# Second attention of a two-layer cross-attention kernel: keys spread over 64 features at a time, scores and maxima products as pairs of 64-row tiles

## The reference, cut to what matters

```python
q = (Q @ Wq_w + Wq_b).reshape(b, tq, H, DK).transpose(0, 2, 1, 3)   # H 16, DK 8
k = (K @ Wk_w + Wk_b).reshape(b, tk, H, DK).transpose(0, 2, 1, 3)
v = (V @ Wv_w + Wv_b).reshape(b, tk, H, DK).transpose(0, 2, 1, 3)
scores = jnp.einsum('bhqd,bhkd->bhqk', q, k) / jnp.sqrt(jnp.float32(DK))
scores = jnp.where(mask == 0, jnp.float32(-1000000000.0), scores)
attn = jax.nn.softmax(scores, axis=-1)
out = jnp.einsum('bhqk,bhkd->bhqd', attn, v)
out = out.transpose(0, 2, 1, 3).reshape(b, tq, c)
return out @ Wo_w + Wo_b
```

## Time and profile before

| what | value |
|---|---|
| median of 3 runs (lowest to highest) | 856.46 us (855.76 to 857.66) |
| profiled execution, its own time | 855.94 us |
| its span, first to last instruction | 854.1 us |
| PE busy / weight loads | 751.2 us (88%) / 625.1 us (73%) |
| DVE, ACT, POOL busy | 598.6 us (70%), 419.9 us (49%), 426.8 us (50%) |
| mean granted TensorE clock, share of full speed | 0.951 |
| second attention | from about 495 us to about 763 us of the span |

### The profile page before, as it was taken

How to read it: one execution, slowest core, us unless ns; L and a number is a source line. 1 busy time by engine, 2 the same in 40 slices (tenths; PEclk the granted TensorE clock), 3 DMA queues, 4 the chain that set the end, 5 groups by cost and what they waited for, 6 DMA issues and landing times. The chain is left out here.

```text
span 854.1 us, 24200 instructions
## 1 busy us (share of the span) xinstructions
PE 751.2 (88%) x9170; PEld 625.1 (73%) x9170; DVE 598.6 (70%) x1658; ACT 419.9 (49%) x847; POOL 426.8 (50%) x464
## 2 busy tenths in 40 slices
PE   3699999999999999999999559999999999966666
PEld 2488878888887888788877437888888888844343
DVE  4576678766876687667864346676776767669996
ACT  2344454445454544444543114555455554537877
POOL 3575557555765567456752043444444444345440
PEclk9799999999999999999999757999999999987988
DMA  9200000000000000000000000000000000000001
GB/s 257 78 2 9 10 10 2 7 7 7 0 7 7 7 0 7 7 7 0 0 2 2 2 11 4 10 6 8 4 4 7 4 7 0 1 2 13 26 25 38
DMA packets 23388, 12.98 MB, mean 15 GB/s; under 512 B 6144, under 2 KB 22480, under 8 KB 23344
## 3 DMA queue, kind: packets, MB, share of 16 engines
q1 hardware_dynamic: 22528, 12.02, 5.2%
q10 hardware_dynamic: 816, 0.36, 0.1%
HBM read 10.28 MB, written 2.10 MB: 14 GB/s over the span
## 5 line engine op out<-in xcount | busy, mean ns | idle before, releaser
L517 POOL TENSOR_TENSOR a_turned<-a_turned,a_rope 128x512 f32<-128x512 f32 x64 | 81.9, 1280 | 166.9 <-DVE a_turned L601 166.9
L745 ACT ACTIVATE a_probs<-bank 77x512 f32<-77x512 f32 x128 | 70.8, 591 | 65.4 <-PE bank L895 64.5
L1462 PE MATMUL bank<-a_q,a_keys 128*128 128x128 f32 x640 | 93.6, 286 | 0.0
L598 DVE TENSOR_TENSOR a_straight<-bank,a_rope 128x512 f32<-128x512 f32 x64 | 44.1, 689 | 61.8 <-PE bank L825 57.3
L518 POOL TENSOR_TENSOR a_qr<-a_straight,a_turned 128x512 f32<-128x512 f32 x64 | 82.3, 1286 | 5.0
L726 ACT COPY a_vs<-bank 77x512 f32<-77x512 f32 x64 | 37.3, 582 | 95.6 <-PE bank L825 95.6
L1462 PEld LDWEIGHTS bank<-a_q,a_keys 128*128 128x128 f32 x640 | 81.1, 196 | 0.1
L626 DVE TENSOR_REDUCE a_am<-bank 128x6 bf16<-128x462 f32 (+1 forms) x96 | 50.3, 581 | 37.6 <-PE bank L869 37.6
L891 PE MATMUL bank<-a_qr,a_kr 64*77 64x128 f32 x1024 | 71.0, 278 | 2.3 <-ACT a_probs L745 0.6
L891 PEld LDWEIGHTS bank<-a_qr,a_kr 64*77 64x77 f32 x1024 | 56.3, 145 | 17.0 <-ACT a_fold L740 9.0
L907 PE MATMUL bank<-a_vs,a_probs 77*64 77x65 f32 x2048 | 66.8, 223 | 0.0
(11 more groups left out here) (226 smaller groups left out, 1965.5 us busy)
## 6 DMA issues: line engine op xcount, KB each, us to landing
a_ctx_in<-in_ctx SPq DMA_DIRECT2D x32, 77.0 KB
out<-x_all SPq DMA_DIRECT2D x8, 256.0 KB, 2.3
x_all<-in_x_dram SPq DMA_DIRECT2D x7, 256.0 KB, 5.8
a_mask_in<-in_mask SPq DMA_DIRECT2D x16, 77.0 KB
a_wq<-in_Wq SPq DMA_DIRECT2D x1, 512.0 KB, 4.9
a_wk<-in_Wk SPq DMA_DIRECT2D x1, 512.0 KB, 6.4
a_wv<-in_Wv SPq DMA_DIRECT2D x1, 512.0 KB, 7.5
a_wo<-in_Wo SPq DMA_DIRECT2D x1, 512.0 KB, 8.7
```

The lines of the kernel that those rows point to most:

```text
L517: steps.link(nc.gpsimd.tensor_tensor(tv, tv, rope[:, 1:2, :].broadcast_to([128, 4, S]), ALU.mult))
L745: nc.scalar.activation(probs[:, 4 * g:4 * g + 4, :], ps[ST_BANK[g]][0:KL, :].rearrange("p (h s) -> p h s", s=S), ACT.Exp).then_inc(s_free[ ...
L1462: nc.tensor.matmul(ps[g][:, (tile % 4) * S:(tile % 4 + 1) * S], keys[P][:, j, 128 * tile:128 * tile + 128], q1[P][:, j, :], start=tile % 4 ...
```

## The change

The mask `BLK` now repeats every 64 features, and `keys` shrinks from 1280 to 640 columns: columns 0 to 511 hold, in features 0 to 63, keys 0 to 63 of heads 0 to 7, and in features 64 to 127 those of heads 8 to 15; columns 512 to 639 do the same for the last 13 keys. The spreads of DVE and POOL and the casts of ACT are over half the columns. Each product of queries and keys now runs over 64 rows, `lo` (features 0 to 63, bank 0) or `hi` (64 to 127, bank 1), and half of bank 2 each. In `score_maxima` the three mask products come first, then the four key products; in `scores` all ten key products come first, then all ten of `fold_w`. A new semaphore `half_done` keeps the two halves from writing bank 2 together.

```diff
-    blk = (rows[:, None] // DK1 == np.arange(H1)[None, :]).astype(np.float32)
+    blk = (rows[:, None] // DK1 % 8 == np.arange(8)[None, :]).astype(np.float32)
...
-    keys = [sb(f"keys{i}", [D, 2, 10 * 128], F32) for i in range(2)]
-    keysb = [sb(f"keysb{i}", [D, 2, 10 * 128], BF16) for i in range(2)]
+    keys = [sb(f"keys{i}", [D, 2, 5 * 128], F32) for i in range(2)]
+    keysb = [sb(f"keysb{i}", [D, 2, 5 * 128], BF16) for i in range(2)]
...
+    FEATURES = (slice(0, D // 2), slice(D // 2, D))
...
         engine.tensor_tensor(
-            keys[P][:, j, 0:1024].rearrange("p (h k) -> p h k", k=KM),
-            k1[:, j:j + 1, 0:KM].broadcast_to([D, H1, KM]),
-            BLK.rearrange("p (h a) -> p h a", a=1).broadcast_to([D, H1, KM]), ALU.mult)
+            keys[P][:, j, 0:512].rearrange("p (h k) -> p h k", k=KM),
+            k1[:, j:j + 1, 0:KM].broadcast_to([D, 8, KM]),
+            BLK.rearrange("p (h a) -> p h a", a=1).broadcast_to([D, 8, KM]), ALU.mult)
         return engine.tensor_tensor(
...
@@ -1439,14 +1440,21 @@
-                nc.tensor.matmul(out, t["identb"][:], mask_cols, start=True, stop=False)
-                nc.tensor.matmul(ps[i][:, 0:cols.stop - cols.start], q1b[P][:, j, :], keysb[P][:, j, cols],
-                                 start=False, stop=True).then_inc(s_full[i], 1)
+                nc.tensor.matmul(out, t["identb"][:], mask_cols, start=True, stop=False, skip_group_check=True)
+            lo, hi = FEATURES
+            nc.tensor.matmul(ps[2][:, 0:128], q1b[P][lo, j, :], keysb[P][lo, j, 512:640],
+                             start=False, stop=True, skip_group_check=True).then_inc(half_done, 1)
+            nc.tensor.matmul(ps[1][:], q1b[P][hi, j, :], keysb[P][hi, j, 0:512],
+                             start=False, stop=True, skip_group_check=True).then_inc(s_full[1], 1)
+            nc.tensor.matmul(ps[0][:], q1b[P][lo, j, :], keysb[P][lo, j, 0:512],
+                             start=False, stop=True, skip_group_check=True).then_inc(s_full[0], 1)
+
+            pe.wait_ge(half_done, 2 * b + 1)
+            nc.tensor.matmul(ps[2][:, 128:256], q1b[P][hi, j, :], keysb[P][hi, j, 512:640],
+                             start=False, stop=True, skip_group_check=True).then_inc(s_full[2], 1)
...
@@ -1456,15 +1464,22 @@
+            def score(g, i, half, tile, first):
+                return nc.tensor.matmul(ps[g][:, i * S:(i + 1) * S], keys[P][FEATURES[half], j, 128 * tile:128 * tile + 128],
+                                        q1[P][FEATURES[half], j, :], start=first, stop=False, skip_group_check=True)
+
+            score(2, 0, 0, 4, True).then_inc(half_done, 1)
+            for i in range(4):
+                score(1, i, 1, i, i == 0)
+                score(0, i, 0, i, i == 0)
+
+            pe.wait_ge(half_done, 2 * b + 2)
+            score(2, 1, 1, 4, False)
+
+            pe.wait_ge(fold_ready, b + 1)
             for g in range(3):
                 tiles = range(4 * g, 4 * g + (4 if g < 2 else 2))
-                for tile in tiles:
-                    nc.tensor.matmul(ps[g][:, (tile % 4) * S:(tile % 4 + 1) * S],
-                                     keys[P][:, j, 128 * tile:128 * tile + 128], q1[P][:, j, :],
-                                     start=tile % 4 == 0, stop=False, skip_group_check=True)
-                if g == 0:
-
-                    pe.wait_ge(fold_ready, b + 1)
```

More of the change, by code:

```diff
@@ L103, in later_weights @@
                    bv=sb("a1_bv", [S, 1, D], F32), bo=sb("a1_bo", [S, 1, D], F32),
-                   fold_w=sb("a1_fold_w", [FOLD, 10, 128], BF16), blocks=sb("a1_blocks", [128, 26], F32),
+                   fold_w=sb("a1_fold_w", [FOLD, 10, 128], BF16), blocks=sb("a1_blocks", [128, 18], F32),
                    mask=sb("a1_mask", [S, KL], I32))
@@ L1038, in layer1_attention @@
     s_full, s_free = [sem(f"s_full{i}") for i in range(3)], [sem(f"s_free{i}") for i in range(3)]
-    m_full, fold_ready, maxima_ready = sem("m_full"), sem("fold_ready"), sem("maxima_ready")
+    m_full, fold_ready, maxima_ready, half_done = sem("m_full"), sem("fold_ready"), sem("maxima_ready"), sem("half_done")
     qk_ready, vals_in, vals_ready = sem("qk_ready"), sem("vals_in"), sem("vals_ready")
@@ L1052, in layer1_attention @@
     HALVES = (slice(0, S // 2), slice(S // 2, S))
-    BLK, HALF, EIGHTH = (blocks[:, 0:16], blocks[:, 16:18], blocks[:, 18:26])
+    BLK, HALF, EIGHTH = (blocks[:, 0:8], blocks[:, 8:10], blocks[:, 10:18])
+    FEATURES = (slice(0, D // 2), slice(D // 2, D))
     def pairs_loop(engine, slot, steps=None, per=0):
@@ L1081, in spread @@
         engine.tensor_tensor(
-            keys[P][:, j, 0:1024].rearrange("p (h k) -> p h k", k=KM),
-            k1[:, j:j + 1, 0:KM].broadcast_to([D, H1, KM]),
-            BLK.rearrange("p (h a) -> p h a", a=1).broadcast_to([D, H1, KM]), ALU.mult)
+            keys[P][:, j, 0:512].rearrange("p (h k) -> p h k", k=KM),
+            k1[:, j:j + 1, 0:KM].broadcast_to([D, 8, KM]),
+            BLK.rearrange("p (h a) -> p h a", a=1).broadcast_to([D, 8, KM]), ALU.mult)
         return engine.tensor_tensor(
-            keys[P][:, j, 1024:1280].rearrange("p (h k) -> p h k", k=RPAD)[:, :, 0:KR],
-            k1[:, j:j + 1, KM:KL].broadcast_to([D, H1, KR]),
-            BLK.rearrange("p (h a) -> p h a", a=1).broadcast_to([D, H1, KR]), ALU.mult)
+            keys[P][:, j, 512:640].rearrange("p (h k) -> p h k", k=RPAD)[:, :, 0:KR],
+            k1[:, j:j + 1, KM:KL].broadcast_to([D, 8, KR]),
+            BLK.rearrange("p (h a) -> p h a", a=1).broadcast_to([D, 8, KR]), ALU.mult)
     front = t["front"]
@@ L1111, in _ @@
         for i in range(2):
-            nc.gpsimd.memset(keys[i][:, :, 1024:].rearrange("p j (h k) -> p j h k", k=RPAD)[:, :, :, KR:], 0.0).then_inc(setup, 1)
+            nc.gpsimd.memset(keys[i][:, :, 512:].rearrange("p j (h k) -> p j h k", k=RPAD)[:, :, :, KR:], 0.0).then_inc(setup, 1)
         nc.gpsimd.memset(ctx8[:], 0.0).then_inc(setup, 1)
@@ L1441, in score_maxima @@
                     out = ps[i][:].rearrange("p (h k) -> p h k", k=KM)
-                    cols = slice(512 * i, 512 * i + 512)
                 else:
@@ L1445, in score_maxima @@
                     out = ps[i][:, 0:256].rearrange("p (h k) -> p h k", k=RPAD)
-                    cols = slice(1024, 1280)
-                nc.tensor.matmul(out, t["identb"][:], mask_cols, start=True, stop=False)
-                nc.tensor.matmul(ps[i][:, 0:cols.stop - cols.start], q1b[P][:, j, :], keysb[P][:, j, cols],
-                                 start=False, stop=True).then_inc(s_full[i], 1)
+                nc.tensor.matmul(out, t["identb"][:], mask_cols, start=True, stop=False, skip_group_check=True)
[9 more added lines that the diff above has]
+                             start=False, stop=True, skip_group_check=True).then_inc(s_full[2], 1)
         def turn_maxima(b):
```

## The result

The changed kernel takes 859.1 us (median of 8 runs, 856.6 to 860.8) where the kernel before takes 855.6 us (8 runs, 853.5 to 857.7): ratio 1.004, 95% interval 1.0023 to 1.0058. It is **slower by 0.4%**; the forecast was 844.1 us, with a range of 834 to 854. The profiled execution has a span of 856.5 us.

A forecast was written before the change was run, and what follows sets the result against it. PE bounds the even slot; in the odd slot the moment bank 0 of the maxima is full decides. Pairs 9.8, stage start 1.3 and first scores 1.2 give 12.3 us off 855.94, 843.6, hence 844.1 us at the median; range 834 to 854.

The forecast's parts named there:

- Part 1: Score products on PE: 64-row pairs with fold_w take 1.91 us instead of 2.91, saving 1.0 us per batch.
- that rival: Score and key products: pairs with 128-column weights do not overlap, so the kernel is slower, 887 us; chance 0.09.
- Part 2: Maxima products on PE: 1.07 us against 1.08, nothing saved, bounds 0.1 us either way.
- Part 3: Halved spread and cast on DVE, POOL, ACT: 0 in steady pairs, 2.3 us at the stage's start.
- The odd slot: Second attention's odd slot: DVE starts 3.98 us behind the scores' start instead of 3.66, a loss of 0.3 us.
- My 2.77 us from DVE to the transposes: Odd slot: time from DVE's first reduction to the transposes, which PE cannot shorten, taken to stay 2.77 us.
- The even slot: Second attention's even slot: PE without a gap, turn_maxima in time by 0.1 us, a gain of 1.0 us.
- The clock: Rival on PE's clock: 1 us more idle time per pair drops it to half, 860 or more; chance 0.03.
- Full gain: Rival: the odd slot follows PE too, 18 us more gain than the forecast, 826; chance 0.07.

The follow-up runs named there:

- e4: Kernel before, with the three mask products of the maxima moved ahead of the three full-row key products; 865.9 us, ratio 1.013.
- e9: Kernel before, with only the maxima's key products as 64-row pairs behind all three masks, scores untouched; 878.2 us, ratio 1.025.
- e10: Kernel before, with score products in 64-row pairs and the three masks ahead of the full-row key products of the maxima; 850.3 us, ratio 0.993.
- e1: Changed kernel plus filler products, 3 behind the odd slot's scores and 7 ahead of the transposes; 847.4 us, ratio 0.991.
- e12: Changed kernel plus 3 filler products ahead of the transposes only; 848.2 us, ratio 0.991.
- e6: Changed kernel plus 6 filler products ahead of the transposes only; 848.2 us, ratio 0.992.
- e2: Kernel before, with only the score products as 64-row pairs, in both slots; 1280-column keys and maxima untouched; 835.1 us, ratio 0.976.
- e8: Changed kernel with the maxima's masks and 64-row key products bank by bank again, one after the other; 855.6 us, ratio 1.001.
- e11: Changed kernel with DVE's normalised rows of the next pair moved ahead of the odd slot's maxima; 839.5 us, ratio 0.981.

## Why the prediction was wrong

**Part 1, right.** The ten score products and `fold_w` take 555.54 - 553.65 = 1.89 us, plus 0.1 us ahead of them; forecast 1.91 for both. Pairs with 128-column weights overlap as those with 77 did, so that rival falls. The factor of two on the Trainium skill's page TensorEngine Tiling (Array Packing), section Theoretical Speedup, would be 1.13 us for the products; they take 1.32 us against 2.25, a factor of 1.7, with the change back to full rows in it.

**Part 2, 0.1 us too low.** These rows are the even slot's, after the change, from its scores on:

```profile
545.98 1.39 PE L1469 MATMUL bank<-a_q,a_keys 64*128 64x128 f32 x20
...
548.89 0.70 PE L1446 MATMUL bank<-s_ampad,identb 128*128 128x512 bf16 x3
549.53 0.23 PE L1448 MATMUL bank<-a_keysb,a_q1b 64*128 64x128 bf16 x1
...
549.97 0.49 PE L1521 MATMUL bank<-a_wo,a_outT 128*128 128x128 f32 x2
550.30 0.61 PE L1533 MATMUL bank<-f_w,a_f_xT 128*128 128x128 f32 x4
...
551.79 0.45 PE L1504 MATMUL bank<-a_vals,a_probs 128*64 128x72 f32 x8
```

The block takes 549.97 - 548.89 = 1.08 us, forecast 1.07. But my sum had the way back to full rows in it, and that comes behind: the output projection takes 550.30 - 549.97 = 0.33 us instead of 0.23. So the edit costs 0.1 us per block, at the edge of my bounds. I took it as neutral; e4, e9 and e10 show that it is the harmful part of the change.

**Part 3, right.** Hidden in the pairs, 1.6 us at the start at a granted clock of 0.50 instead of 0.62; in e1, at 0.64, this stretch takes 11.8 us, 2.4 us less than before, where I had 2.3. With the scores of the first slot the stage's third pair starts 2.1 us earlier (530.9 instead of 533.0); the sum had 2.5 us.

**The odd slot, right.** Forecast a loss of 0.3 us, measured 0.31 (from `values_rows` to the next transposes 7.86 us instead of 7.55, at full clock). The agreement is partly luck: DVE starts at 3.87 where it started at 3.65 in the same pair before, so it is 0.22 us late and not 0.32, and the other 0.09 us are the change into 64 rows ahead of the scores. My 2.77 us from DVE to the transposes came from an early pair; in this one they are 2.91 us, before and after.

**The even slot, too high by 0.4 us.** The gain of 1.0 us was mis-sized; it measured 0.63 us. The step is "`turn_maxima` is at 6.16. In time by 0.1 us". I compared it with the row maxima and overlooked the third thing that it waits for, `f_done`, DVE's addition of the feed-forward product, which stands behind the maxima in DVE's order. The row at 552.42 names it. It starts 0.63 us behind the last `values` products (551.79), where this took 0.38 us before, so it is 0.25 us late: at 6.44 us behind the scores' start instead of 6.19. The way back to full rows of Part 2 is the other 0.1 us. A pair gains 0.3 us instead of 0.7: 14 x 0.4 = 5.6 us less.

**The clock, wrong: the step that failed.** The forecast put it at nothing. The rival had a chance of 0.03 and a price of "860 or more", and it is what happened. The evidence that I held against it was no evidence. That the last stage had the full clock with 58% busy is a mean over ten microseconds and says nothing of one place in the order; and "PE stays near 90%" came true (182.05 of 200 us) with the clock at 0.95. The runs show in its place a clock that falls in six of 13 pairs around the wait for `xhat`, 1.5 us each, and stays full when three products fill this wait (e12).

The account of the two profiled executions is this. With the change the third pair starts 2.14 us earlier. From there to the last transposes it needs 202.93 us instead of 198.07, 4.86 more: six falls cost 9.0 us, the shorter pairs give back 4.1. What is behind them is 0.32 us shorter, with the seventh fall in it. -2.14 + 4.86 - 0.32 = 2.4 us, the difference of the two spans (856.5 and 854.1). Without the falls the measured terms give 855.6 - 14 x 0.33 - 2.1 = 848.9 us, inside my range; e6 and e12, which only prevent them, take 848.2. So of the 15 us between forecast and result the clock is about 10 and the even slot about 5, and the clock alone decides the sign.

**The chances.** Full gain needed the odd slot to follow PE. It can: e2 gains 1.4 us per pair. I had looked for the gain in the change as it stood and not asked which of its parts carries it; the sum made for "only the scores" ahead of e2 had bank 0 at 3.1 us and 838 to 842 us, 2 to 6 us below my forecast, and e2 measured 9 us below it.

**Still open.** Why the maxima's 64-row pairs ahead of a 0.8 us wait let the clock fall often, why the scores' pairs do it rarely and full-row products not at all, and what brought the one fall of e8 without this wait. The runs tell some of the conditions, not the mechanism. Whether e2 with the rows of e11 would be faster still was not tried.

## What to carry to other kernels

A faster engine in front of a chain that it does not end does not shorten the chain: ask for each part of a change when the first consumer's data are complete, and keep what a slow consumer starts on (here bank 0) ahead of everything that waits. List every semaphore of the next waiting instruction, the ones of other stages too. And when PE gets idle time at one place of a tightly packed loop, look at the granted clock pair by pair; a few products that fill the wait, or work moved off the path, can be worth more than the work that was saved.

## What the runs showed of the hardware

- After the change the clock fell to half around waits of 0.78 to 0.83 us (0.61 us in the last pair), in a stage where PE was busy for 91% of the time, in about every second pair. With 0.33 us of bf16 filler in the wait it did not fall in the steady pairs (e12: 1.00 over 200 us).
- The same wait without any 64-row products in the second attention left the clock alone (e4: 1.00); with 64-row pairs in the maxima it fell often (e9: 0.94 over 200 us), with pairs in the scores only, once (e10: 0.99). At waits of 0.57 to 0.62 us pairs in the scores did not bring it down (e2).
- A change between full-row and 64-row products costs 0.1 us in either direction (e8). Around the maxima's pairs there are two; the pairs take 0.44 us (549.53 to 549.97) where 1280 columns took 0.54, so the block is 0.1 us longer and not shorter.
- Adding products made a kernel faster: 859.1 to 847.4 us with ten fillers per pair (e1).
